# Grouped attention: the output projection as three float32r products per chunk, its operands split by ScalarE and GpSimd

## The chip, the cores and the metric

The kernel runs on one core of a Trainium2 chip. Its engines are TensorE (PE in the profile; its weight loads stand apart as PEld), VectorE (DVE), ScalarE (ACT), GpSimd (POOL) and SyncE (SP, which issues the DMAs). The metric is the device time of one execution in microseconds, as the median of several runs. Lower is better.

## The reference

Sixteen batches of 128 tokens with 256 features pass through six layers, each with a layer norm ahead of it and a residual behind it: causal attention, cross attention, a gated MLP, grouped attention, masked cross attention, and an MLP with quantised operands. The change is in the fourth, `_L1_attn_ref`:

```
D_MODEL, H, G = (256, 32, 8)          # 32 heads of 8 features, 8 groups of keys and values
Q = x @ Wq + bq ; K = x @ Wk + bk ; V = x @ Wv + bv
scores = einsum(Q, K) / sqrt(D_K) ; attn = softmax(scores) ; out = einsum(attn, V)
return out @ Wo + bo                  # the product that the change touches
```

## The kernel before

`grouped_attention` runs between 803 and 995 us of the profiled execution. Each engine has its own program, a function `step(t, s)` that is called for t from -2 to 17. Step t of TensorE works on several batches at once: it projects queries, keys and values of batch t+1, makes the scores of batch t, turns the maxima of the scores (`turn_maxima`, L2623), weighs the values (`weigh_values`, L2652), turns the output of batch t-1 (`turn_out`, L2681, and `turn_heads`, L2695), and projects the heads of batch t-2 (`project_heads`, L2703). The order on each engine is written out by hand; engines wait for each other through semaphores that count batches, and an engine that waits holds up all that stands behind in its own order.

`project_heads(b)` is out @ Wo for one batch: 128 tokens by 256 features, summed over two chunks (EC = 2) of 128 features. Its stationary operand is `headsT`, the turned heads in SBUF, and its moving operand is `wo`. Both are float32, and TensorE's records show each float32 product as two passes (four records in a batch). The path of a batch through it is this:

- VectorE `normalise_heads` (L2544 and L2546) divides by the sums and writes `heads`.
- TensorE `turn_heads` (L2695) turns them into PSUM (`bank_misc`, upper half).
- ScalarE `copy_headsT` (L2458) copies them to SBUF in the same step, t = b+1.
- TensorE `project_heads` (L2703) runs in step t = b+2, behind `turn_maxima(t, s, 1)` and ahead of `turn_out`.
- VectorE `update_x` (L2555) adds the product to x, and `statistics` (L168 to L172) of that batch follow a step later.

On ScalarE a step ends with `own_queries` (L2421) and the next one begins with `copy_keys` (L2439), which waits for TensorE's projections of keys and queries (L2657). On GpSimd a step begins with `add_bias` (L2383), then `narrow_q` (L2367), which waits for ScalarE's queries (L2413), and `narrow_own_keys` (L2375). The last batch, 15, passes `turn_heads` in step 16 and `project_heads` in step 17. Then all engines meet and `masked_cross_attention` begins, with products of weights on TensorE (L1801, then L1806).

In other layers of the same kernel products are already made from float32r halves: an operand is rounded to float32r by ScalarE (high), the rest is what a subtraction leaves (low), and the product is high*high + high*low + low*high. `PARTS = ((0, 0), (0, 1), (1, 0))` lists these pairs.

Of the kernel before, what the change touches and what calls it, by code (L numbers as in the profile page):

```python
# [5 lines left out]
F32 = mybir.dt.float32  # L6
BF16 = mybir.dt.bfloat16
F32R = mybir.dt.float32r
I32 = mybir.dt.int32
HIGH_BITS = -(1 << 12)  # L10
ALU = mybir.AluOpType
ACT = mybir.ActivationFunctionType
AX = mybir.AxisListType

P = 128
# [5 lines left out]
PARTS = ((0, 0), (0, 1), (1, 0))  # L21
EMBED = 256
EC = EMBED // P
# [4 lines left out]
def nonneg(count):  # L28

    return max(count, 0) if isinstance(count, int) else count  # L30
# [72 lines left out]
class Layer:  # L103
# [17 lines left out]
    def sbuf(self, name, shape, dtype=F32):  # L121
        return self.ctx.enter_context(self.nc.sbuf_tensor(f"{self.name}_{name}", shape, dtype))

    def sem(self, name):

        self.used += 1
        return self.core.semaphores[self.parity][self.used - 1]
# [160 lines left out]
def batch_there(b):  # L288
    return not isinstance(b, int) or 0 <= b < BATCHES
# [1984 lines left out]
def grouped_attention(nc, core, dram, next_weights):  # L2274
# [11 lines left out]
    with ExitStack() as ctx:  # L2286
# [25 lines left out]
        reciprocal = sbuf("reciprocal", [P, HEADS])  # L2312
        heads = sbuf("heads", [P, HEADS, D])
        headsT = sbuf("headsT", [P, EC, P])

        bank_scores, bank_scoresT, bank_out, bank_misc = core.banks[0:2], core.banks[2:6], core.banks[6], core.banks[7]
        turned_maxima = [bank_scoresT[0][:, 0:P], bank_scores[0][:, 0:P]]
# [10 lines left out]
        out_filled, outT_ready, out_turned = sem("out_filled"), sem("outT_ready"), sem("out_turned")  # L2328
        heads_chain, heads_ready = sem("heads_chain"), sem("heads_ready")
        headsT_filled, headsT_ready = sem("headsT_filled"), sem("headsT_ready")  # L2330
        left = Statistics(layer, "left", BATCHES - LEFT_BY_QUAD)
        block = ctx.enter_context(nc.Block())

# [18 lines left out]
        @block.gpsimd  # L2352
        def _(pool):
            for s in range(2):
                pool.memset(values[s][:, :], 0.0)
                last = pool.memset(maxima[s][:, :, :, :], 0.0)
            last.then_inc(constants_ready, 1)
            pool.wait_ge(constants_ready, 1)
            for s in range(2):
                last = pool.memset(values_of(s, D, 1), 1.0)  # L2360
            last.then_inc(constants_ready, 1)
            pool.wait_ge(core.constants_loaded, CONSTANTS)

            def narrow_q(b, s):
                pool.wait_ge(q_ready, b + 1)
                pool.wait_ge(scores_filled, nonneg(GROUPS * (b - 1)))
                pool.tensor_tensor(qT_bf[s][:, :, :], qT[:, :, :],  # L2367
                                   core.ones[:, 0:1].unsqueeze(2).to_broadcast([P, EC, P]), ALU.mult)\
                    .then_inc(q_bf_ready, 1)

            def narrow_own_keys(b, s):
                pool.wait_ge(k_ready, b + 1)
                pool.wait_ge(scores_filled, nonneg(GROUPS * (b - 1)))
                for m in range(PER):
                    last = pool.tensor_tensor(kT_bf[s][:, :, m, :], kT[s][:, :, :],  # L2375
                                              own[:, m:m + 1].unsqueeze(2).to_broadcast([P, EC, P]), ALU.mult)
                last.then_inc(k_bf_ready, 1)

            def add_bias(b):

                pool.wait_ge(bias_ready, 1)
                pool.wait_ge(layer.h_ready, b + 1)
                pool.tensor_tensor(core.batch_x(b), core.batch_x(b), bias[:, :], ALU.add).then_inc(bias_added, 1)  # L2383

            def step(t, s):
                if batch_there(t + 1):
                    if t + 1 > 0:
                        add_bias(t + 1)
                    narrow_q(t + 1, 1 - s)
                    narrow_own_keys(t + 1, 1 - s)  # L2390
                    if t + 1 == 0:
                        add_bias(t + 1)
                if batch_there(t - 3) and not left_to_next(t - 3):
                    layer.pool_rstd(pool, t - 3, STATISTICS_STEPS)
                if isinstance(t, int) and t == -1:
                    left.pool_rstd(pool, LEFT_BY_QUAD)
            batches(pool, step)

        @block.scalar
        def _(act):  # L2400
# [53 lines left out]

            def copy_headsT(b):
                act.wait_ge(headsT_filled, b + 1)
                act.wait_ge(layer.y_filled, nonneg(b))
                act.activation(headsT[:, :, :], bank_misc[:, EMBED:2 * EMBED].rearrange("p (c t) -> p c t", c=EC),  # L2458
                               ACT.Copy).then_inc(headsT_ready, 1)

            def normalise(b):
                act.wait_ge(layer.hT_filled, nonneg(b))
# [8 lines left out]
            last.then_inc(wide_ready, 1)  # L2471

            def step(t, s):
                if batch_there(t + 1):
                    copy_keys(t + 1, 1 - s)
                    copy_queries(t + 1)
# [114 lines left out]
        def _(pe):  # L2591
# [105 lines left out]
                last.then_inc(headsT_filled, 1)  # L2697

            def project_heads(b):
                pe.wait_ge(headsT_ready, b + 1)  # L2700
                y = bank_misc[:, 0:EMBED]
                for c in range(EC):
                    last = pe.matmul(y, headsT[:, c, :], wo[:, c, :], start=(c == 0), stop=(c == EC - 1))  # L2703
                last.then_inc(layer.y_filled, 1)

            def step(t, s):
# [531 lines left out]
```

## Time and profile before

| | us |
|---|---|
| median of 3 runs | 1536.37 (1535.61 to 1536.84) |
| the profiled execution | 1536.67 |
| its span in the trace | 1534.4 |
| TensorE busy | 1454.1 (95%) |
| VectorE busy | 1115.4 (73%) |
| ScalarE busy | 978.9 (64%) |
| GpSimd busy | 734.3 (48%) |

TensorE is close to always busy, yet its share says little about one stage: its products are pipelined, so that records overlap, and a step can be bound by a loop through two engines while TensorE's idle time in it looks small. The profiled execution takes 2.3 us more than its span, for what lies around the first and the last instruction. The DMA engines are all but idle in the middle of the stage.

### The profile page before, as it was taken

To read this page: it belongs to the slowest core of one execution; us is meant where nothing else is said; L and a number is where in the kernel's file an instruction comes from. 1 tells how busy PE (TensorE), PEld (TensorE's weight loads), DVE (VectorE), ACT (ScalarE), POOL (GpSimd) and SP (SyncE) were. 2 spreads that over 40 slices of the span, in tenths; PEclk is the share of its full clock that TensorE was granted. 3 is DMA by queue.
4 is the path that set the end of the run, shared out by engine and by line. 5 is a ranking of instruction groups with operands and counts; after the bars stand their busy time and mean duration, and the time that the engine had idled before them with its cause. 6 is when DMAs were issued, how large, how long until landed. Compare 5 with 4: busy or idle time off the path is not lost. (4 is left out here: it accounts for less than half of the span.)

```text
span 1534.4 us, 30706 instructions
## 1 busy us (share of the span) xinstructions
PE 1454.1 (95%) x10384; PEld 1206.1 (79%) x10384; DVE 1115.4 (73%) x2539; ACT 978.9 (64%) x2620; POOL 734.3 (48%) x899
## 2 busy tenths in 40 slices
PE   5999889999999999899998999899999999989998
PEld 2666678888888888688875555489999999867887
DVE  4888668888888887554545777656777777688887
ACT  2777567777777777432325888677777787742222
POOL 3766545555555555232333433213444444457765
PEclk9999999999999999999998999999999999999999
DMA  6000020000000000000003000020000000000000
GB/s 251 2 2 2 15 87 3 5 3 3 5 3 5 4 3 1 23 1 1 1 7 132 1 2 1 9 103 8 9 8 9 8 2 2 1 1 15 14 11 18
DMA packets 15612, 29.84 MB, mean 19 GB/s; under 512 B 1506, under 2 KB 12003, under 8 KB 14691
## 3 DMA queue, kind: packets, MB, share of 16 engines
q1 hardware_dynamic: 15458, 27.89, 5.0%
q8 instruction: 85, 1.39, 0.4%
q14 instruction: 69, 0.56, 0.1%
HBM read 25.79 MB, written 2.10 MB: 18 GB/s over the span
## 5 line engine op out<-in xcount | busy, mean ns | idle before, releaser
L1468 POOL TENSOR_TENSOR weights_even<-weights_even,cross_reciprocal 128x512 f32<-128x512 f32 x64 | 66.7, 1042 | 187.4 <-DVE cross_reciprocal L1720 187.4
L945 POOL TENSOR_TENSOR cross_work<-cross_work,cross_reciprocal 128x512 f32<-128x512 f32 x64 | 66.6, 1040 | 174.8 <-DVE cross_reciprocal L1102 174.8
L1168 PE MATMUL bank<-ident,cross_work 128*128 128x128 f32 x768 | 117.3, 275 | 2.5 <-DVE cross_work L1080 2.2
L998 ACT ACTIVATE cross_work<-bank,cross_shift,cross_q_rms 128x128 f32<-128x128 f32 x256 | 113.6, 456 | 5.2 <-DVE cross_shift L1074 4.5
L1168 PEld LDWEIGHTS bank<-ident,cross_work 128*128 128x128 f32 x768 | 89.9, 141 | 30.1 <-DVE cross_work L1080 21.2
L2525 DVE TENSOR_REDUCE grouped_maxima<-bank 128x4 bf16<-128x512 f32 x128 | 82.3, 685 | 36.4 <-PE bank L2606 36.4
L2001 POOL TENSOR_TENSOR mlp_low_inner<-mlp_inner,mlp_high_inner 128x512 fp32r<-128x512 f32 x36 | 48.7, 1353 | 117.6 <-ACT mlp_high_inner L2044 117.6
L1557 ACT ACTIVATE weights_even<-bank,cross_shift 128x128 f32<-128x128 f32 x256 | 90.4, 366 | 11.1 <-DVE cross_shift L1712 10.0
L1710 DVE TENSOR_REDUCE cross_maxima<-bank 128x4 f32<-128x512 f32 x64 | 44.1, 689 | 71.8 <-PE bank L1854 71.8
L2878 ACT ACTIVATE mx_silu<-bank 128x512 f32<-128x512 f32 x32 | 19.1, 598 | 113.3 <-PE bank L3028 113.3
L404 POOL TENSOR_TENSOR causal_masked_maxima<-causal_maxima,causal_constants 128x512 bf16<-128x512 bf16 x64 | 66.5, 1060 | 46.5 <-DVE causal_maxima L552 42.1
L1193 PE MATMUL bank<-high_weights,cross_high 128*128 128x512 f32 x192 | 87.0, 453 | 0.0
L2404 ACT ACTIVATE grouped_probs<-bank 128x512 f32<-128x512 f32 x128 | 69.9, 606 | 23.5 <-PE bank L2639 23.5
L1885 PE MATMUL bank<-cross_high_wo,cross_high_heads 128*128 128x256 f32 x256 | 76.2, 298 | 8.0 <-DVE cross_low_heads L1699 7.8
L986 ACT ACTIVATE cross_high_probsT<-bank 128x512 fp32r<-128x512 f32 x64 | 38.4, 599 | 67.7 <-PE bank L1168 67.7
L2100 DVE SCALAR_TENSOR_TENSOR mlp_gated<-mlp_tanh,bank 128x512 f32<-128x512 f32 x36 | 24.7, 687 | 77.5 <-ACT mlp_tanh L2038 71.9
L1836 PE MATMUL bank<-cross_high_hT,late_high 128*128 128x256 f32 x256 | 78.0, 305 | 0.7 <-ACT weights_even L1550 0.7
L1258 PE MATMUL bank<-cross_high_wo,cross_high_heads 128*128 128x256 f32 x256 | 77.1, 301 | 0.0
L1193 PE MATMUL bank<-low_weights,cross_high 128*128 128x512 f32 x192 | 76.6, 399 | 0.0
L1193 PE MATMUL bank<-high_weights,cross_low 128*128 128x512 f32 x192 | 76.6, 399 | 0.0
L1885 PE MATMUL bank<-cross_high_wo,cross_low_heads 128*128 128x256 f32 x256 | 72.3, 282 | 0.0
L1885 PE MATMUL bank<-cross_low_wo,cross_high_heads 128*128 128x256 f32 x256 | 72.3, 282 | 0.0
(382 smaller groups left out, 5362.2 us busy)
## 6 DMA issues: line engine op xcount, KB each, us to landing
weights_even<-in_weights SPq DMA_DIRECT2D x2, 2560.0 KB, 11.6
weights_even<-in_weights SPq DMA_DIRECT2D x2, 1732.0 KB, 8.5
weights_odd_early<-in_weights SPq DMA_DIRECT2D x1, 3072.0 KB, 11.8
weights_odd_values<-in_weights SPq DMA_DIRECT2D x1, 3072.0 KB, 18.8
weights_odd_late<-in_weights SPq DMA_DIRECT2D x2, 1536.0 KB, 9.5
x<-in_x SPq DMA_DIRECT2D x4, 512.0 KB, 8.0
out<-mx_result SPq DMA_DIRECT2D x16, 128.0 KB, 1.7
weights_even<-in_weights SPq DMA_DIRECT2D x2, 512.0 KB, 5.8
```

The costliest lines, as they stand in the source:

```text
L404: pool.tensor_tensor(masked_maxima[g][:, :, :], maxima[s][:, g, :].unsqueeze(2).to_broadcast([P, PER, P]), later.unsqueeze(1).to_broadcast ...
L945: pool.tensor_tensor(probs[x], probs[x], reciprocal[x][:, :].unsqueeze(2).to_broadcast([P, PER, P]), ALU.mult).then_inc(probs_divided, 1)
L998: last = act.activation(probs[x][:, j, :], bank_scores[:, j * P:(j + 1) * P], ACT.Exp, scale=q_rms[x][:, j:j + 1], bias=shift[x][:, j:j + ...
L1168: last = pe.transpose(bank[:, j * P:(j + 1) * P], source, core.ident[:, :])
L1193: last = pe.matmul(out, half[:, c, :], split_weights[b][:, at:at + PER * D], start=(k == 0), stop=(k == len(jobs) - 1))
L1258: last = pe.matmul(bank_y[:, 0:EMBED], heads[x][a][:, j, :], wo_split[c][:, h, :], start=(g == 0 and m == 0), stop=(g == GROUPS - 1 and m ...
L1468: pool.tensor_tensor(probs[x], probs[x], reciprocal[x][:, :].unsqueeze(2).to_broadcast([P, JOBS, P]), ALU.mult).then_inc(probs_divided, 1)
L1557: last = act.activation(probs[x][:, j, :], bank_scores[x][:, j * P:(j + 1) * P], ACT.Exp, scale=SCALE, bias=shift[x][:, j:j + 1], accum_ou ...
L1836: last = pe.matmul(bank_q[:, j * BOTH * P:(j + 1) * BOTH * P], wqk_split[b][:, c, h * D:(h + 1) * D], hT[s][a][:, c, :, :].rearrange("p b ...
L1885: last = pe.matmul(bank_y[s][:, k * EMBED:(k + 1) * EMBED], heads[x][a][:, k * PER + j, :], wo_split[b][:, g * PER + j, :], start=(g == 0 ...
L2404: act.activation(probs[:, SLOTS * c + j, :], bank_scoresT[j][:, :], ACT.Exp, scale=SCALE)\
L2525: dve.tensor_reduce(maxima[s][:, c, 2 * pair + j, 0:PER], bank_scores[j].rearrange("p (h k) -> p h k", h=PER), AX.X, ALU.max).then_inc(max ...
```

## The change

The edit adds four SBUF tensors (high and low halves of the turned heads and of `wo`, in float32r) and four semaphores. ScalarE rounds `wo` once at the start of step 0 and GpSimd subtracts it at the start of step 1. For each batch ScalarE rounds `headsT` from SBUF at the start of step b+2, ahead of that step's `copy_keys`; GpSimd subtracts at the start of the same step, ahead of `add_bias` and `narrow_q`; TensorE's `project_heads(b)` waits for GpSimd and makes six float32r products in place of two float32 ones. `copy_headsT` waits for the previous subtraction in place of the previous product.

```diff
+        headsT_split = [sbuf(f"{half}_headsT", [P, EC, P], F32R) for half in ("high", "low")]
+        wo_split = [sbuf(f"{half}_wo", [P, EC, EMBED], F32R) for half in ("high", "low")]
...
+            def low_wo():
+                pool.wait_ge(wo_high, 1)
+                pool.tensor_tensor(wo_split[1][:, :, :], wo, wo_split[0][:, :, :].bitcast(F32), ALU.subtract)\
+                    .then_inc(wo_low, 1)
+
+            def low_headsT(b):
+                pool.wait_ge(headsT_high, b + 1)
+                pool.tensor_tensor(headsT_split[1][:, :, :], headsT[:, :, :], headsT_split[0][:, :, :].bitcast(F32),
+                                   ALU.subtract).then_inc(headsT_low, 1)
+
             def step(t, s):
+                if isinstance(t, int) and t == 1:
+                    low_wo()
+                if batch_there(t - 2):
+                    low_headsT(t - 2)
                 if batch_there(t + 1):
...
             def copy_headsT(b):
                 act.wait_ge(headsT_filled, b + 1)
-                act.wait_ge(layer.y_filled, nonneg(b))
+                act.wait_ge(headsT_low, nonneg(b))
...
+            def round_headsT(b):
+                act.wait_ge(headsT_ready, b + 1)
+                act.wait_ge(layer.y_filled, nonneg(b))
+                act.activation(headsT_split[0][:, :, :], headsT[:, :, :], ACT.Copy).then_inc(headsT_high, 1)
...
             def step(t, s):
+                if isinstance(t, int) and t == 0:
+                    act.activation(wo_split[0][:, :, :], wo, ACT.Copy).then_inc(wo_high, 1)
+                if batch_there(t - 2):
+                    round_headsT(t - 2)
                 if batch_there(t + 1):
                     copy_keys(t + 1, 1 - s)
...
             def project_heads(b):
-                pe.wait_ge(headsT_ready, b + 1)
+                if isinstance(b, int) and b == 0:
+                    pe.wait_ge(wo_low, 1)
+                pe.wait_ge(headsT_low, b + 1)
                 y = bank_misc[:, 0:EMBED]
-                for c in range(EC):
-                    last = pe.matmul(y, headsT[:, c, :], wo[:, c, :], start=(c == 0), stop=(c == EC - 1))
+                jobs = [(c, x, w) for c in range(EC) for x, w in PARTS]
+                for m, (c, x, w) in enumerate(jobs):
+                    last = pe.matmul(y, headsT_split[x][:, c, :], wo_split[w][:, c, :],
+                                     start=(m == 0), stop=(m == len(jobs) - 1))
                 last.then_inc(layer.y_filled, 1)
```

## Rows read from the trace of the kernel before

**Rows 1.** Windows: us, busy (records) of PE, PEld, DVE, ACT, POOL, then PEclk, DMA.

```profile
915.00:935.00 20.00, 19.57 (x157) 10.31 (x155) 15.77 (x37) 16.20 (x41) 8.28 (x14) 1.00 0.01 2
```

**Rows 2.** Timeline of TensorE, one step: start, duration, line, tiles, count, idle time.

```profile
919.60 0.22 PE L2623 MATMUL bank<-minus_ident_bf,grouped_maxima 128*128 128x128 bf16 x1
919.66 1.08 PE L2703 MATMUL bank<-weights_odd_late,grouped_headsT 128*128 128x256 f32 x4
920.58 0.60 PE L2681 MATMUL bank<-ident,grouped_outT 128*128 128x128 f32 x4
922.50 0.44 PE L2687 MATMUL bank<-ident,grouped_h 128*128 128x128 f32 x2
922.77 0.38 PE L2695 MATMUL bank<-ident,grouped_heads 128*128 128x128 f32 x2
...
930.19 0.22 PE L2623 MATMUL bank<-minus_ident_bf,grouped_maxima 128*128 128x128 bf16 x1
```

**Rows 3.** Timeline of VectorE, the same step.

```profile
919.86 0.69 DVE L2534 TENSOR_TENSOR grouped_shifts<-bank,grouped_columns 128x512 bf16<-128x512 f32 x1 [0.33 <-PE bank L2623]
...
921.50 0.42 DVE L2555 TENSOR_TENSOR x<-x,bank 128x256 f32<-128x256 f32 x1
...
922.23 0.42 DVE L2546 TENSOR_TENSOR grouped_heads<-bank,grouped_reciprocal 128x256 f32<-128x256 f32 x1
```

**Rows 4.** Timeline of ScalarE and of GpSimd, where the added work goes.

```profile
925.18 0.95 ACT L2421 ACTIVATE grouped_q_own<-grouped_qT,grouped_columns 128x256 f32<-128x256 f32 x2
926.73 0.62 ACT L2439 ACTIVATE grouped_kT<-bank,grouped_columns 128x128 f32<-128x128 f32 x2 [0.60 <-issue]
...
927.95 0.61 POOL L2367 TENSOR_TENSOR grouped_qT_bf<-grouped_qT,ones 128x256 bf16<-128x256 f32 x1 [5.15 <-ACT grouped_qT L2413]
```

**Rows 5.** One line each: a split of 128x256 by ScalarE and GpSimd elsewhere.

```profile
L1581 ACT ACTIVATE cross_high_context<-cross_context x8: 412/427/434, 1010.4 to 1270.1; 128x256 fp32r<-128x256 f32 x8
L1497 POOL TENSOR_TENSOR cross_low_context<-cross_context,cross_high_context x8: 725/730/734, 1010.9 to 1297.6; 128x256 fp32r<-128x256 f32 x8
```

**Rows 6.** Timeline of TensorE, 256-column float32r products of another layer.

```profile
1102.93 0.38 PE L1885 MATMUL bank<-cross_high_wo,cross_high_heads 128*128 128x256 f32 x1
1103.16 0.28 PE L1885 MATMUL bank<-cross_low_wo,cross_high_heads 128*128 128x256 f32 x1
...
1103.87 0.28 PE L1885 MATMUL bank<-cross_low_wo,cross_high_heads 128*128 128x256 f32 x1
```

**Rows 7.** Timeline of ScalarE at the stage's start.

```profile
821.87 0.62 ACT L2439 ACTIVATE grouped_kT<-bank,grouped_columns 128x128 f32<-128x128 f32 x2 [3.84 <-issue]
```

**Rows 8.** Timeline of TensorE and ScalarE, step 16, batch 14.

```profile
989.24 1.13 PE L2703 MATMUL bank<-weights_odd_late,grouped_headsT 128*128 128x256 f32 x4
989.46 0.60 ACT L2446 ACTIVATE grouped_outT<-bank 128x512 f32<-128x512 f32 x1 [1.26 <-PE bank L2652]
```

**Rows 9.** Timeline of three engines, batch 15 and the next layer's start.

```profile
992.25 0.38 ACT L2458 ACTIVATE grouped_headsT<-bank 128x256 f32<-128x256 f32 x1 [2.20 <-PE bank L2695]
992.69 1.13 PE L2703 MATMUL bank<-weights_odd_late,grouped_headsT 128*128 128x256 f32 x4 [0.47 <-ACT grouped_headsT L2458]
993.92 0.42 DVE L2555 TENSOR_TENSOR x<-x,bank 128x256 f32<-128x256 f32 x1 [1.33 <-issue]
994.92 1.35 PE L1801 MATMUL bank<-weights_even 128*128 128x128 f32 x10 [1.09 <-DVE x L2555]
```

**Rows 10.** Windows around a fall of the clock, and around this stage's end.

```profile
800.40:804.20 3.80, 1.74 (x13) 1.56 (x14) 1.63 (x5) 0.81 (x3) 1.06 (x4) 1.00 0.00 0
804.20:811.00 6.80, 6.80 (x24) 5.46 (x24) 0.00 (x0) 1.14 (x4) 0.21 (x3) 0.50 0.96 371
992.00:995.40 3.40, 1.83 (x10) 1.19 (x9) 1.36 (x10) 0.45 (x2) 0.65 (x2) 1.00 0.00 0
995.40:1002.20 6.80, 6.80 (x63) 6.80 (x63) 4.82 (x10) 5.48 (x13) 0.00 (x0) 1.00 0.79 249
```

**Rows 11.** Timeline of TensorE inside the stretch at the half clock.

```profile
807.67 3.57 PE L2657 MATMUL bank<-grouped_hT,weights_odd_late 128*128 128x128 f32 x16
```

More of the change, by code:

```diff
@@ L2330, in grouped_attention @@
         headsT_filled, headsT_ready = sem("headsT_filled"), sem("headsT_ready")
+        headsT_high, headsT_low = sem("headsT_high"), sem("headsT_low")
+        wo_high, wo_low = sem("wo_high"), sem("wo_low")
         left = Statistics(layer, "left", BATCHES - LEFT_BY_QUAD)
```

## The prediction

> **What bounds the kernel now.** I read the busy time by stretch first, then the timelines of one step in the middle of the stage, engine by engine, then those of its two ends, and last the granted clock around the stage's borders. The stretch in the middle shows TensorE busy 19.57 of 20 us at the full clock, VectorE 15.77, ScalarE 16.20 [rows 1]. That looks like a stage bound by TensorE, in which every saved product pays. The timeline says something else. A step lasts 10.59 us (`turn_maxima` starts at 919.60 and again at 930.19), and in it `project_heads` starts at 919.66 and the next thing at 920.58, so the product costs 0.92 us of TensorE's time [rows 2]. But VectorE starts a run of work at 919.86, released by that same `turn_maxima` ahead of the product: shifts, statistics, `update_x` at 921.50, the reciprocal, and the heads from 922.23 to 922.65 [rows 3]. `turn_heads` needs those heads and starts at 922.77, right behind `turn_h`, which started at 922.50 [rows 2]. So two chains arrive there almost together: TensorE's own, and VectorE's, which begins at `turn_maxima` and doesn't contain the product. The reader is to see that the wait is hidden in the rows because both are in step, not because VectorE is early: TensorE's second product of `turn_h` began about 0.11 us before 922.77, so VectorE's 922.65 left under 0.12 us minus the semaphore's way.
>
> **The product.** Four passes of 0.92 us go. Six float32r products of the same 256 columns come: six intervals of such a series take 1103.87 - 1103.16 = 0.71 us when it runs, and with the slower first interval 1103.87 - 1102.93 = 0.94 us for seven, or some 0.82 for six [rows 6]. I take 0.76 us, a saving of 0.16 us a step on TensorE (0.10 to 0.21). Then `turn_out`, the scores and `turn_h` all come 0.16 us earlier and `turn_heads` stands waiting for heads at 922.65, which haven't moved: `update_x` is held by the statistics ahead of it on VectorE, not by the product. What gets through is only what TensorE lost between the heads' arrival and 922.77. Bounds: 0, and the whole 0.16. The heads' end and that start are 0.12 us apart, and a semaphore takes part of that (0.05 us from the copy's end at 992.64 to the product at 992.69 [rows 9]), so I take 0.015 us a step, over some 13 full steps 0.2 us gained; the upper end is 13 x 0.16 = 2.1 us.
>
> **The rounding and the subtraction, in full steps.** ScalarE's round of 128x256 from SBUF takes 0.43 us and GpSimd's subtraction 0.73 us [rows 5]. The round goes behind `own_queries` (two in 0.95 us, done at 926.13) and ahead of `copy_keys`, before which ScalarE idles 0.60 us [rows 4]; since operations overlap by about a tenth, it occupies 0.40 and ends near 926.5, with `copy_keys` still at 926.73. Behind it on ScalarE stand the keys, the queries and the exponentials; if the cover were gone each would be later by the excess, and GpSimd's `narrow_q` and TensorE's scores with them. The subtraction runs from 926.55 to 927.3 in GpSimd's idle 5.15 us before `narrow_q` at 927.95 [rows 4]. Its other new waits (the previous `y_filled`, the previous low half) were met a step before. TensorE's wait for the low half comes at 930.25, 3 us later. I charge nothing; between 0 and 0.2 us a step is what I can't exclude. SP's queue and its DMAs aren't passed or changed. `wo` is split once: ScalarE idles 3.84 us before the keys in step 0 [rows 7], which hides a 128x512 round (estimate from the 128x256 one: at most 0.86), and GpSimd's subtraction (at most 1.46, by the same doubling) has its wait before the next `narrow_q`.
>
> **The end of the stage: batch 14.** ScalarE idles 1.26 us until `copy_outT` at 989.46 [rows 8]. The round starts as that idle time does, near 988.0 to 988.2 with its overlap, and takes 0.43; the subtraction's 0.73 [rows 5] ends between 989.1 and 989.4, and TensorE reaches the product at 989.24 [rows 8]: no delay, or 0.2 us that the product's own saving pays back. In these last steps TensorE and ScalarE, not VectorE, set the pace, so the 0.16 us saved on batch 13 does arrive: another 0.2 us gained.
>
> **The end of the stage: batch 15.** Nothing stands beside it. Now: the copy ends at 992.64, the product starts at 992.69 and its result is there at 993.82, VectorE adds at 993.92, the next layer's first product starts at 994.92 [rows 9]. After: copy to 992.64, round 0.43 with 0.05 ahead of it to 993.12, GpSimd 0.07 + 0.73 to 993.92, then 0.05, and six products with a cold start: five starts after the first at 0.23 + 4 x 0.118 = 0.70, and 0.28 for the last [rows 6], so 0.98, to 994.95. That is 1.1 us later than 993.82 (0.9 to 1.3), and everything behind it moves by that.
>
> So far: -0.2 - 0.2 + 1.1 = +0.7 us.
>
> **The clock behind that gap.** The granted clock stays at 2.4 GHz here: TensorE is busy 1.83 of 3.40 us in 992.0 to 995.4 and the next 6.8 us are at 1.00 [rows 10]. At the stage's other border it was busy 1.74 of 3.80 us (800.4 to 804.2), and the next 6.8 us ran at half, 1.2 GHz [rows 10]. The change stretches the same border: between `turn_heads`' end (992.2) and the next layer at 994.92 + 1.1 = 996.0, TensorE would have 0.98 us of records in 3.8 us where it had 1.13 in 2.7. That is less than it did ahead of that fall (26% of the time against 46%, where it now has 54%), so I expect a fall. Its price: at half the 16 products of 128 columns take (3.57 - 0.37)/15 = 0.21 us each [rows 11], in the next layer (1.35 - 0.35)/9 = 0.11 [rows 9]. TensorE is busy 6.80 of 6.80 us there [rows 10], so nothing hides it: 6.8 us at half do the work of 3.5, a loss of 3.3 us, less up to half of the idle 1.1 us if the fall comes ahead of the restart (2.7 to 3.3). I take 3.2.
>
> The Trainium skill ("TensorE: Matmul & The Clock Gate", section "HAM oscillation — how this bites in real kernels") speaks of a re-throttle only for idle gaps longer than any in this border, so by it there is no fall and the sum stays at +0.7. This trace disagrees: ahead of the fall at 804.2 the 1.74 us of busy time left TensorE no such gap either.
>
> **Sum.** 1536.67 (the profiled execution, 1534.4 of span and 2.3 around it) + 0.7 + 3.2 = 1540.6. The median of the runs is 0.3 below the profiled execution, so 1540.3.
>
> **Rivals.**
> - *No fall of the clock.* The same schedule, with the next layer at 2.4 GHz throughout: 1536.37 + 0.7 = 1537.1 (1536.6 to 1537.6), no measurable change. For it: the clock held at this very border before [rows 10], and one other border is thin evidence. Against it: this border becomes emptier than that one. It decides at the next layer's first products, which cost 0.11 us each or 0.21. This is my case on the other side, not slower.
> - *TensorE's saving counts.* If the heads were there in time after all, 13 steps give 0.16 each: 1537.1 - 1.9 = 1535.2, still within the noise; at 0.21 a step and no fall 1534.6. For it: TensorE's 19.57 of 20 us [rows 1]. Against it: VectorE's chain starts ahead of the product [rows 3].
> - *The cover is too thin.* ScalarE's keys slip, by some 0.2 us a step (a round that takes 0.80 in place of 0.43, or products that come with more than the 0.12 us of rows 6): 13 x 0.2 = 2.6 us on top, 1542.9. Against it: 0.60 us of idle time for 0.40 of work, and the exponentials wait for TensorE behind it anyway.
>
> **How the numbers follow.** The forecast gets 0.66 with 1539.3 to 1541.1 as its own range, no fall 0.23, the saving 0.05, the thin cover 0.06. A measurement of this kernel tells 0.2%, 3.1 us, from no change. Of the forecast about a tenth lies under +3.1 (a tail of 0.9 and a price of 2.7), so slower gets 0.60 + 0.05 = 0.65; the same 0.23 + 0.06 + 0.03 = 0.32; faster 0.03. The range takes in both clock cases: 1536.4 (no fall and a small tail) to 1541.6.
>
> **What would show it.** In the step: six records of `project_heads` in about 0.76 us, then an idle time before `turn_heads` with VectorE's heads as its releaser, and the step still 10.57 to 10.59 us; an even 10.43 would prove the saving counts. ScalarE's idle time before `copy_keys` falls from 0.60 to about 0.2 and no more. At the end: the product of batch 15 at about 994.0, the next layer at about 996.0, and a granted clock of 0.5 for 6.8 us near its start. With the clock at 1.00 there, the forecast is wrong and the first rival right; with steps over 10.7 us, the third.

## The result, and the profile after

The changed kernel takes 1541.38 us in the median of 20 runs (1537.18 to 1543.29). The kernel before, run beside it, takes 1536.85 us (20 runs, 1532.49 to 1540.28). The ratio of the two is 1.0026, 95% interval 1.0018 to 1.0034: slower by 0.26%, little but clear of the noise. The forecast was 1540.3.

The first view is TensorE's timeline of one full step (start, duration, engine, line, tiles, shape, count, idle time before):

```profile
921.12 0.22 PE L2650 MATMUL bank<-minus_ident_bf,grouped_maxima 128*128 128x128 bf16 x1
921.15 0.36 PE L2733 MATMUL bank<-grouped_high_wo,grouped_high_headsT 128*128 128x256 f32 x1
921.35 0.28 PE L2733 MATMUL bank<-grouped_low_wo,grouped_high_headsT 128*128 128x256 f32 x1
...
921.83 0.28 PE L2733 MATMUL bank<-grouped_high_wo,grouped_low_headsT 128*128 128x256 f32 x1
921.95 0.60 PE L2708 MATMUL bank<-ident,grouped_outT 128*128 128x128 f32 x4
923.87 0.44 PE L2714 MATMUL bank<-ident,grouped_h 128*128 128x128 f32 x2
924.23 0.44 PE L2722 MATMUL bank<-ident,grouped_heads 128*128 128x128 f32 x2
924.60 1.06 PE L2679 MATMUL bank<-grouped_probs,grouped_values 128*32 128x512 f32 x8
925.60 0.39 PE L2633 MATMUL bank<-grouped_kT_bf,grouped_qT_bf 32*128 32x512 bf16 x2
925.91 1.60 PE L2684 MATMUL bank<-grouped_hT,weights_odd_late 128*128 128x128 f32 x12
927.40 0.23 PE L2650 MATMUL bank<-minus_ident_bf,grouped_maxima 128*128 128x128 bf16 x1
...
931.67 0.22 PE L2650 MATMUL bank<-minus_ident_bf,grouped_maxima 128*128 128x128 bf16 x1
```

The product takes 921.95 - 921.15 = 0.80 us where it took 0.92 [rows 2], and `turn_h` comes 0.15 us sooner behind `turn_maxima` (2.75 us for 2.90). But `turn_heads` now comes 0.36 us behind `turn_h`, where it was 0.27. (The profile prints no idle time there, because the records of `turn_h` end only at 924.31; the wait is read from the starts.) The step is 931.67 - 921.12 = 10.55 us for 10.59. VectorE in the same step:

```profile
921.38 0.69 DVE L2561 TENSOR_TENSOR grouped_shifts<-bank,grouped_columns 128x512 bf16<-128x512 f32 x1 [0.32 <-PE bank L2650]
...
923.03 0.42 DVE L2582 TENSOR_TENSOR x<-x,bank 128x256 f32<-128x256 f32 x1
923.37 0.35 DVE L2571 RECIPROCAL grouped_reciprocal<-bank 128x32 f32<-128x32 f32 x1
923.75 0.42 DVE L2573 TENSOR_TENSOR grouped_heads<-bank,grouped_reciprocal 128x256 f32<-128x256 f32 x1
924.09 1.28 DVE L2552 TENSOR_REDUCE grouped_maxima<-bank 128x4 bf16<-128x512 f32 x2
```

It hasn't moved: 1.65 us from the shifts to `update_x`, as in 921.50 - 919.86 = 1.64 before [rows 3]. The heads are ready at 923.75 + 0.42 = 924.17, and `turn_heads` follows at 924.23. ScalarE and GpSimd take the added work in idle time (the first two lines are ScalarE's, the last three GpSimd's):

```profile
927.36 0.45 ACT L2482 ACTIVATE grouped_high_headsT<-grouped_headsT 128x256 fp32r<-128x256 f32 x1
928.22 0.62 ACT L2457 ACTIVATE grouped_kT<-bank,grouped_columns 128x128 f32<-128x128 f32 x2 [0.41 <-issue]
...
927.89 0.73 POOL L2396 TENSOR_TENSOR grouped_low_headsT<-grouped_headsT,grouped_high_headsT 128x256 fp32r<-128x256 f32 x1 [4.26 <-ACT grouped_high_headsT L2482]
928.57 0.73 POOL L2387 TENSOR_TENSOR x<-x,grouped_bias 128x256 f32<-128x256 f32 x1
929.44 0.61 POOL L2371 TENSOR_TENSOR grouped_qT_bf<-grouped_qT,ones 128x256 bf16<-128x256 f32 x1
```

At the end of the stage nothing covers it. In order of time, four engines:

```profile
995.02 0.41 PE L2722 MATMUL bank<-ident,grouped_heads 128*128 128x128 f32 x2 [1.00 <-DVE grouped_heads L2573]
995.46 0.38 ACT L2476 ACTIVATE grouped_headsT<-bank 128x256 f32<-128x256 f32 x1 [2.17 <-PE bank L2722]
995.88 0.42 ACT L2482 ACTIVATE grouped_high_headsT<-grouped_headsT 128x256 fp32r<-128x256 f32 x1
996.37 0.72 POOL L2396 TENSOR_TENSOR grouped_low_headsT<-grouped_headsT,grouped_high_headsT 128x256 fp32r<-128x256 f32 x1 [3.32 <-ACT grouped_high_headsT L2482]
997.15 0.58 PE L2733 MATMUL bank<-grouped_high_wo,grouped_high_headsT 128*128 128x256 f32 x1 [1.72 <-POOL grouped_low_headsT L2396]
...
998.38 0.41 PE L2733 MATMUL bank<-grouped_high_wo,grouped_low_headsT 128*128 128x256 f32 x1
998.89 0.42 DVE L2582 TENSOR_TENSOR x<-x,bank 128x256 f32<-128x256 f32 x1 [3.10 <-issue]
999.88 1.41 PE L1801 MATMUL bank<-weights_even 128*128 128x128 f32 x5 [1.09 <-DVE x L2582]
```

From `turn_heads` to the next layer's first product it is 999.88 - 995.02 = 4.86 us, where it was 994.92 - 991.81 = 3.11. The turn in the kernel before (its copy and what follows are in [rows 9]):

```profile
991.81 0.41 PE L2695 MATMUL bank<-ident,grouped_heads 128*128 128x128 f32 x2 [1.00 <-DVE grouped_heads L2546]
```

In the changed kernel the products here are 0.21 us apart and not 0.12: the clock falls at 997.2, as they begin. The windows (us, busy and records of PE, PEld, DVE, ACT, POOL, then PEclk, DMA share, GB/s):

```profile
993.80:997.20 3.40, 0.68 (x5) 0.25 (x3) 1.89 (x9) 0.80 (x2) 0.83 (x2) 1.00 0.00 0
997.20:1004.00 6.80, 5.71 (x25) 5.45 (x26) 1.87 (x7) 1.52 (x3) 0.50 (x2) 0.50 0.34 87
1004.00:1010.00 6.00, 6.00 (x55) 5.97 (x54) 4.46 (x8) 4.60 (x12) 0.00 (x0) 1.00 0.99 374
```

TensorE was busy 0.68 of 3.40 us at 2.4 GHz; then come 6.8 us at 1.2 GHz. Before, at this border, it was busy 1.83 of 3.40 and kept 2.4 GHz [rows 10].

The two profiled executions differ by 7.1 us of span. Of that 2.0 lies ahead of the stage (its first `turn_maxima` is at 822.83 for 820.85). 0.3 of it is there by 26 us, and the rest goes with a stretch of 3.4 us at half clock at 171 us that only the changed kernel's execution had; the edit changes nothing there, so this is chance. The stage, from that `turn_maxima` to the next layer, is 177.05 us for 174.07. Of these 3.0 us the border is 1.75, and the full steps give some 0.5 back. Most of what is left comes from another fall, 6.8 us long, at 980.1: in step 15 the second `turn_maxima` follows the first by 5.62 us where it was 4.01. The profiled execution of the kernel before has no fall there, though the same kernel with other small edits does (e2, e5, e11). Behind the stage 541.6 us remain to the end of the span for 539.5. And the time around the span is 1.8 us (1543.27 less 1541.5), where it was 2.3.

### The profile page after: what moved, and what is told of

It reads as the page before. It is cut to its first block and busy times, and to the rows that moved or that the text cites. A ratio compares the mean times of both kernels' runs of the same rounds, so it can differ in the third digit from the quotient of the medians.

```text
span 1541.5 us, 30821 instructions
## 1 busy us (share of the span) xinstructions
PE 1461.0 (95%) x10416; PEld 1210.4 (79%) x10416; DVE 1116.0 (72%) x2539; ACT 984.3 (64%) x2637; POOL 748.0 (49%) x916
```

## The experiments

The runs come in four groups, the changed kernel's and three of experiments (e1, e2, e3 and e7; e4, e5, e6 and e8; e9 to e12), the last of them on another chip than the two before it. The kernel before was run in each, and the ratios in the table are to those runs. Its means in the groups are 1536.9, 1537.6, 1537.4 and 1537.4 us, so where an experiment is set against the changed kernel, which is in a group of its own, up to 0.7 us can come from that.

One kernel's executions spread over 4 to 13 us. Most of that goes with one quantity that every run lists: from its granted clock c the time at half clock is 2 x (1 - c) x span. Over the 234 executions for which the clock is listed, of all kernels, one slope fits: each us at half clock goes with 0.26 us of time, with 1.2 us left over. So the table gives a mean time at equal half clock beside the median, with twice its standard error; it is a fit, not a measurement. Two things blur it. The clock's record begins 13 to 26 us into an execution, and what is ahead of it isn't counted: in all 14 profiles the products of 512 columns between 18 and 22 us come 0.85 us apart, as at half clock (0.43 from 30 us on), but only the ten records that begin by 15 us count a stretch there. And the time around the span is 1.8 us for the changed kernel, e1 to e4 and e7 to e10 (2.0 for e6), but 2.3 for the kernel before, e5, e11 and e12: 0.5 us that belongs to no step. By spans alone the changed kernel stands at +1.0 and not +0.5. "Step" is the period of `turn_maxima` in the middle, "border" the time from the last `turn_heads` to the next layer's first product, "rest" from there to the end of the span; these three are of the profiled execution.

```
kernel                          runs  median   ratio (95%)             step   border  rest    at half, mean  equal half, to before
before                            88  1537.27                          10.59  3.11    539.5   31.7            0
changed                           20  1541.38  1.0026 (1.0018-1.0034)  10.55  4.86    541.6   41.7           +0.5 (0.6)
e1 last batch float32             12  1539.54  1.0016 (1.0003-1.0028)  10.56  3.10    540.2   39.0            0.0 (0.7)
e2 before, split of batch 15      11  1540.54  1.0020 (1.0009-1.0032)  10.59  4.36    541.2   36.9           +1.5 (0.7)
e3 TensorE kept busy              12  1537.70  1.0005 (0.9993-1.0018)  10.56  4.40    540.0   32.5           +0.5 (0.7)
e7 all splits, float32 products   12  1540.47  1.0020 (1.001-1.003)    10.59  4.35    542.5   35.6           +1.8 (0.7)
e6 products without splits        12  1540.33  1.0012 (0.9997-1.0028)  10.56  2.95    542.7   40.5           -0.4 (0.7)
e4 changed, heads first            6  1547.21  1.0061 (1.004-1.0081)   11.06  4.20    541.2   37.6           +7.8 (1.0)
e5 before, heads first             7  1545.42  1.0050 (1.0032-1.0068)  11.20  3.11    539.7   33.1           +7.6 (0.9)
e8 e4 with e1                      6  1545.74  1.0050 (1.003-1.007)    11.06  3.11    541.1   39.6           +6.4 (1.0)
e9 changed, statistics cut        12  1538.96  1.0009 (0.9995-1.0023)  10.47  4.21    541.3   36.4           -0.1 (0.7)
e11 before, statistics cut        12  1537.83  0.9998 (0.9984-1.0013)  10.62  3.10    539.8   32.0           +0.1 (0.7)
e12 before, last steps kept busy  12  1537.67  1.0001 (0.9987-1.0015)  10.59  3.11    539.5   31.0            0.0 (0.7)
e10 e9 + e1 + e12                 12  1536.18  0.9994 (0.9982-1.0006)  10.47  3.30    539.9   33.8           -1.7 (0.7)
```

**e1: the changed kernel, batch 15 by the old products.** The serial split at the border is gone; all else stays. (In the diffs from here on, notes behind # are added, and conditions that only pick the steps are not shown.)

```diff
-                if batch_there(t - 2):
+                if batch_there(t - 2) and t - 2 != BATCHES - 1:    # round_headsT and low_headsT
...
+                if b == BATCHES - 1:                               # project_heads: the two float32 products
```

> The changed kernel, but batch 15 alone goes the old way: two float32 products straight from headsT, no round and no subtraction for it. Theory (serial end plus clock): the 1.2 us between the last copy_headsT and the last product shrink to 0.05, the border looks as it did before the change, the clock falls there as seldom as before, and the time is that of the kernel before, less 0.4 to 0.7 us: ratio to before 0.9990 to 1.0005. Rival (the loss is spread over the steps, through the added ScalarE and GpSimd work): the time stays that of the change, 1.0025 to 1.0035 of before.

The border is back at 3.10 us and the clock holds behind it (rest 540.2). The median comes 1.8 us down, not all the way to the kernel before: the ratio's interval, 1.0003 to 1.0028, lies above what was expected. This kernel still had 7.3 us more at half clock than the kernel before (95% interval 2.8 to 11.8), and not measurably less than the changed kernel (2.7, interval -2.5 to 8.0).

**e2: the kernel before, with the round, the subtraction and the wait for batch 15 alone; its products stay float32.** The split of `wo` at the stage's start stays in too.

```diff
+                if t - 2 == BATCHES - 1:       # ScalarE: round_headsT, GpSimd: low_headsT
+                if b == BATCHES - 1:           # TensorE
+                    pe.wait_ge(headsT_low, 1)
```

> The kernel before (float32 products everywhere), but for batch 15 alone ScalarE rounds headsT, GpSimd subtracts, and the product, still float32 from headsT, waits for that; its results are not used. Theory: the last product starts 1.2 us later, at 993.9 by the clock of the trace before, the next layer 1.2 us later, and the clock falls to 1.2 GHz near that point in most executions for 6.8 us: +1.2 without a fall, +4.4 with one, a median of +3.5 to +4.5 us. Rival (only the serial work costs, the clock's falls are chance): a median of +1.2 us and falls at that place no more often than before.

One operation more on each of two engines, at the end of the stage, costs 1.25 us at the border (4.36 for 3.11) and is followed by a fall (3.4 us long, rest 541.2). The split of `wo` costs next to nothing: one early step is 0.05 us longer. The median is 3.1 us above that of the kernel before in the same group, most of what the whole change costs. The time at half clock is 5.3 us longer (interval 1.5 to 9.1), which by the fit is 1.4 us of it. Its chain, to compare with [rows 9]:

```profile
993.27 0.42 ACT L2482 ACTIVATE grouped_high_headsT<-grouped_headsT 128x256 fp32r<-128x256 f32 x1
993.76 0.72 POOL L2396 TENSOR_TENSOR grouped_low_headsT<-grouped_headsT,grouped_high_headsT 128x256 fp32r<-128x256 f32 x1 [5.63 <-ACT grouped_high_headsT L2482]
994.54 1.13 PE L2734 MATMUL bank<-weights_odd_late,grouped_headsT 128*128 128x256 f32 x4 [1.72 <-POOL grouped_low_headsT L2396]
995.77 0.42 DVE L2582 TENSOR_TENSOR x<-x,bank 128x256 f32<-128x256 f32 x1 [2.59 <-issue]
996.77 4.41 PE L1801 MATMUL bank<-weights_even 128*128 128x128 f32 x24 [1.09 <-DVE x L2582]
```

**e3: the changed kernel, with TensorE kept busy at the border** by transposes that nothing reads.

```diff
+                if t == BATCHES + 1:
+                    keep_busy(14)
                 if batch_there(t - 2):
                     project_heads(t - 2)
+                if t == BATCHES + 1:
+                    keep_busy(8)
```

> The changed kernel, with 14 transposes of the identity on TensorE ahead of the wait for the last product and 8 behind it, into a bank that nobody reads any more: they fill the idle time and do nothing for the output. Theory: the last product still starts 1.2 us late (the 14 take 1.55 us of the 1.7 that TensorE waits), but the clock no longer falls at this border: +0.5 to +1.2 us against before, 3 less than the change; the profile shows 1.00 from 990 to 1005. Rival (the falls come from elsewhere): no shorter than the change, +4 to +5 us.

The serial chain is all there (border 4.40, where e9 below has 4.21 at full clock), yet the clock stays up. TensorE's timeline, then the windows:

```profile
994.32 1.69 PE L2728 MATMUL bank<-ident 128*128 128x128 f32 x14
...
996.20 0.39 PE L2737 MATMUL bank<-grouped_high_wo,grouped_high_headsT 128*128 128x256 f32 x1 [0.20 <-POOL grouped_low_headsT L2396]
...
997.02 1.04 PE L2728 MATMUL bank<-ident 128*128 128x128 f32 x8
998.47 2.80 PE L1801 MATMUL bank<-weights_even 128*128 128x128 f32 x23 [0.41 <-PEq L2286]
```

```profile
993.00:996.40 3.40, 2.20 (x18) 1.93 (x18) 1.74 (x9) 0.80 (x2) 0.97 (x2) 1.00 0.00 0
996.40:999.80 3.40, 2.99 (x26) 2.78 (x26) 1.18 (x6) 0.76 (x2) 0.35 (x2) 1.00 0.06 16
```

Against the changed kernel the median falls by 3.7 us (the means by 2.4, 95% interval 1.0 to 3.9), although the transposes add 0.2 us to the border; each set against the kernel before of its own group, the means differ by 3.1. At equal half clock it stands where the changed kernel does, +0.5; the whole gain is in the clock, 9.2 us less at half. So it is shown that the clock costs this kernel time and that work at the border gives it back, by an edit that takes no work away. It isn't shown that the split alone brings the falls: e1, which takes the split away, keeps 6.4 us more at half clock than e3 (interval 0.9 to 12.0).

**e7: the changed kernel's splits with the old products.**

```diff
-                jobs = [(c, x, w) for c in range(EC) for x, w in PARTS]
...
+                for c in range(EC):
+                    last = pe.matmul(y, headsT[:, c, :], wo[:, c, :], start=(c == 0), stop=(c == EC - 1))
```

> The changed kernel with all its rounds, subtractions and waits, but the two float32 products from headsT and wo in place of the six; the halves are made and not used. Theory: the step lasts as before, 10.59 us (10.58 to 10.60), since ScalarE and GpSimd do the new work in idle time; the end of the stage costs 1.2 to 1.3 us and the clock falls there: +3.5 to +5 us against before. Rival (rounding and subtracting slow the steps): a step of 10.65 us or more.

The step is 10.59, as before the change, with all rounding and subtracting in it: the cover is complete. The border is 4.35, as in e2, and so is the time: 3.0 us over the kernel before in the median, a little less than expected, with 4.0 us more at half clock (interval 0.8 to 7.1).

**e6: the changed kernel's six products without the splits.** The stationary operand is a half of `wo`; this leaves the values of the turned heads out of the output.

```diff
-                    last = pe.matmul(y, headsT_split[x][:, c, :], wo_split[w][:, c, :],
+                    last = pe.matmul(y, wo_split[x][:, c, 0:P], wo_split[w][:, c, :],
```

> The six float32r products alone: no round and no subtraction per batch, the stationary operands are taken from the split wo (in place of the turned heads, whose values this leaves out of the output), and the product waits for copy_headsT as before. Theory: the step is that of the change, 10.55 us, so the per-batch splitting is free in the steps; the end has no added 1.2 us, the last product ends 0.2 us sooner than before, and the clock falls at the border as in the kernel before: -0.6 to -1.0 us against before. Rival (per-batch splitting costs in the steps): a step shorter than 10.50 us.

The step is 10.56 and the border 2.95, 0.16 us shorter than before: there the shorter product arrives in full. The median is 3.1 us over the kernel before (the ratio's interval, 0.9997 to 1.0028, just reaches 1), where 0.6 to 1.0 us less was expected, with 8.8 us more at half clock (interval 4.4 to 13.3). Its profile has a fall at the border although the border is short. So the serial split isn't the only thing that brings falls here: the short products alone go with more of them, and the expectation had nothing for that.

**e4 and e5: VectorE's heads ahead of its statistics,** in steps up to 14, in the changed kernel and in the kernel before, to take away the wait of `turn_heads`.

```diff
-                if batch_there(t - 3) and not left_to_next(t - 3):
-                    statistics(t - 3)
                 if batch_there(t - 2):
                     update_x(t - 2)
                 if batch_there(t - 1):
                     normalise_heads(t - 1)
+                if batch_there(t - 3) and not left_to_next(t - 3):
+                    statistics(t - 3)
```

> The changed kernel with VectorE's order turned in steps up to 14: update_x and normalise_heads ahead of the statistics. The heads come some 0.9 us earlier. Theory (TensorE's saved 0.16 us a step is absorbed by the wait for the heads): now it counts, the step goes from 10.55 to 10.42 to 10.45 us, and the time is 1.3 to 1.7 us less than the change. Rival (something else bounds the step): the step stays at 10.55.

> The kernel before with the same order of VectorE as in the heads-first kernel, float32 products. Theory: TensorE's own chain already reaches turn_heads at the same moment as the heads did, so earlier heads bring nothing: a step of 10.57 to 10.59 us and the time of before within 0.4 us. Rival (VectorE alone bounds the step): the step falls below 10.5 us here too.

Both are slower by 8 us and more, which the expectations missed. VectorE in e4:

```profile
922.72 0.42 DVE L2582 TENSOR_TENSOR x<-x,bank 128x256 f32<-128x256 f32 x1 [0.58 <-ACT grouped_values L2447]
...
923.44 0.42 DVE L2573 TENSOR_TENSOR grouped_heads<-bank,grouped_reciprocal 128x256 f32<-128x256 f32 x1
...
924.82 1.29 DVE L2552 TENSOR_REDUCE grouped_maxima<-bank 128x4 bf16<-128x512 f32 x2
```

`update_x` isn't free until 922.72: it also waits for ScalarE's copy of the values (L2447), and that copy waits for the product. So VectorE idles 0.58 us in the place of the statistics, and these then stand ahead of the row maxima, which end at 926.11. TensorE waits for them (0.58 us idle before its next scores at 926.17). In the changed kernel the statistics fill just that idle time. The pair does show one thing well: where `update_x` waits for that copy, the product is in VectorE's chain. The copy starts 1.32 us behind `turn_maxima` in e5 and 1.18 in e4, and 11.20 - 11.06 = 0.14 us of the saving arrive in each step. And with the heads early TensorE reaches `turn_heads` by itself 3.18 us behind `turn_maxima` with the float32 product (e5) and 3.03 with the new one (e4); in the kernel before and the changed kernel the distances are 3.17 and 3.11. TensorE's way was the later one before, VectorE's is now.

**e8: e4 with e1.** 

> Heads-first order together with the old way for batch 15: the step's saving counts and the end costs nothing. Theory: 13 steps x 0.15 us saved, the end as before: -2.0 to -2.6 us against before, falls of the clock at the border as often as in the kernel before, and faster than both kernels. Rival: no better than the old way for batch 15 alone (-0.4 to -0.7).

The border is 3.11 and the time stays as slow as the step. The expectation, faster than both kernels, missed with e4's. Against e4 it is 1.5 us less both in the medians and at equal half clock, near the border's 4.20 - 3.11 = 1.09.

**e9 and e11: only the first instruction of the statistics stays ahead,** the short ones go behind the next row maxima; in the changed kernel and in the kernel before.

```diff
                 if batch_there(t - 3) and not left_to_next(t - 3):
-                    statistics(t - 3)
+                    first_statistics(t - 3)
...
                 if batch_there(t + 1):
                     row_maxima(t + 1, 1 - s, 0, 0)
+                if batch_there(t - 3) and not left_to_next(t - 3):
+                    rest_of_statistics(t - 3)
```

> The changed kernel, with VectorE's statistics of batch t-3 cut in two in the full steps: only their first instruction stays ahead of update_x, the short ones go behind the next row maxima. Theory: in the changed kernel a step is set by VectorE's unbroken run from turn_maxima over the shifts, statistics, update_x and the heads to the row maxima (3.11 us to turn_heads); update_x could start 0.31 us sooner (922.72 for 923.03, as with the heads first), the row maxima end earlier, and the next bound is TensorE's own way with the shorter product, 3.03 us. So the step goes from 10.55 to 10.47 us, 1.0 us over the stage, 1539.5 to 1540.5 in all. Rival: the product's saving can't pass at all, because ScalarE or the keys set the step: it stays at 10.55. Other rival: the short instructions behind the row maxima delay the next ones, as whole statistics there did: 10.6 or more.

> The kernel before with the same cut of the statistics. Theory: there the float32 product stands on TensorE's own way to turn_heads and to ScalarE's copies (3.17 us, 3.18 with the heads first), so that earlier heads give nothing: the step stays at 10.58 to 10.60 us, ratio 0.999 to 1.001. With e9 this is a table of two by two: only where both are done does the step fall to 10.47. Rival: VectorE sets the step in the kernel before already, and it falls by 0.08 there too.

The step is 10.47 in e9, as forecast to the hundredth, and 10.62 in e11. TensorE in e9:

```profile
919.32 0.22 PE L2671 MATMUL bank<-minus_ident_bf,grouped_maxima 128*128 128x128 bf16 x1
...
922.07 0.44 PE L2735 MATMUL bank<-ident,grouped_h 128*128 128x128 f32 x2
922.35 0.38 PE L2743 MATMUL bank<-ident,grouped_heads 128*128 128x128 f32 x2
```

`turn_heads` comes 922.35 - 919.32 = 3.03 us behind `turn_maxima`, right behind `turn_h`. The same edit gives -0.08 us with the shorter product and +0.03 with the long one: each shortens one of two parallel ways, and only both together shorten the step. (e11's 0.03 are more than I expected; there the next row maxima start 0.06 us later behind the scores than in the kernel before, 0.51 for 0.45.) At the border, here wholly at 2.4 GHz, it is 4.21: 1.10 us more than before. The median, 1538.96, is half a us below what was expected; the run isn't shown to be slower than the kernel before, nor faster.

**e12: the kernel before, with TensorE kept busy in steps 15 and 16.**

```diff
+                if t == BATCHES - 1:
+                    pe.wait_ge(headsT_ready, t - 1)
+                    keep_busy(bank_misc, 12)
+                if t == BATCHES:
+                    keep_busy(bank_scores[1], 8)
```

> The kernel before, with transposes that nothing reads in TensorE's idle time of the last steps: 12 in step 15 where the projections were, 8 at the start of step 16. Theory: most executions have a stretch at 1.2 GHz that begins 976 to 984 us in, behind this thinner step; with TensorE kept busy it goes, for 1.5 to 2.5 us on the median, less 0.2 for the longer step 15: ratio 0.9985 to 1.000. Rival: the stretches come at about a fixed distance from the earlier ones, whatever TensorE does here: one is still seen between 976 and 984 us and the ratio is 1.000 to 1.001.

No fall is seen between 976 and 988 us, and none in e10 either, where ten of the twelve other profiles have one (the kernel before and e7 don't). Yet neither median nor time at half clock moved (31.0 for 31.7), and the ratio is the rival's. One profile without a fall doesn't show that the transposes took one away, since the profile of the kernel before has none there either.

**e10: the changed kernel with e9, e1 and e12 together.**

> What the runs so far point to, together: the changed kernel with batch 15 by float32 products (no serial split at the border), the statistics cut in two, and the transposes of e12. Theory: step 10.47, the border as in the kernel before (2.65 us from the copy of batch 15 to the next layer), fewer stretches at 1.2 GHz: 1.6 us less by steps, up to 2 by the clock, so 1533.5 to 1536, ratio 0.9975 to 0.9990 to the kernel before. Rival: the stretches go elsewhere, and it is at 1536 to 1538.

It has the lowest median, 1536.18, 5.2 us under the changed kernel (the means 4.3, 95% interval 3.1 to 5.5), but not the 1536 or less that was expected; it lies where the rival put it. Against the kernel before its interval, 0.9982 to 1.0006, still reaches over 1, so it isn't shown to be faster. At equal half clock it is 1.7 us better, about what the shorter steps (13 x 0.12 us) make. Its border is 3.30 and not 3.11: the next layer's first product comes 1.19 us behind `update_x` and not 1.00, for a reason that no run shows.

## Why the prediction was right, point by point

- **The product, 0.76 us for 0.92.** Nearly. It is 0.80: the first interval is 0.20 us and the others 0.12. The saving is 0.12 to 0.15 us.
- **TensorE's saving stops at the heads: 0.015 us a step.** Right in mechanism: `turn_heads` follows the heads by 0.06 us in the changed kernel, and e9 shows that it is they that hold the rest. The size was under: 0.04 us. I had read one chain too few. In the kernel before, the keys' projection waits for ScalarE's copy of the turned heads, behind exponentials that themselves stand behind the product (the copy ends at 924.37, the projection starts at 924.51). In the changed kernel that copy starts 4.22 us behind `turn_maxima`, where it was 4.36, and the projection no longer waits for it: it follows the scores ahead of it by 0.31 us, where it was 0.42. With that way shorter, VectorE's, just behind it, took over. Over the stage this is some 0.5 us against my 0.2.
- **The splits cost nothing in full steps.** Right: 10.59 in e7, 10.56 in e6 and 10.55 with both. ScalarE still idles 0.41 us ahead of the keys, where I expected 0.2.
- **Batch 14, 0.2 us gained.** Nearly: from `turn_maxima` of step 15 to `turn_heads` of batch 15 the distance is 8.88 us before (982.92 to 991.81), 9.00 with the splits alone (e7), and 8.77 and 8.78 in e1 and e3: 0.1 gained. The splits take 0.1 here, and the products pay it back.
- **Batch 15, +1.1 us.** Right: 1.10 at full clock (e9). With the float32 product it is 1.25 (e2). In the profiled execution of the changed kernel it is 1.75, because the clock fell ahead of the product: the other 0.65 us belong to the next item.
- **The fall behind the border, 3.2 us.** The profile has it where I put it, 6.8 us long. Its size there: rest is 539.5 to 540.2 us in the seven profiles without a fall there (before, e1, e3, e5, e10, e11, e12), 541.1 to 541.3 in four with 3.4 us (e2, e4, e8, e9) and 542.5 and 542.7 in two with 6.8 (e7, e6). So 6.8 us at half cost about 2.7 (2.3 to 3.2), 3.4 us about 1.4, and not each execution has the long form. In the changed kernel it is 2.1 behind the next layer's start and 0.65 ahead of it, also near 2.7. I had 3.2, with TensorE busy through all of the 6.8 us; it was busy for 5.71 of them. (A price holds for its place: e5 and e12 have a fall of 3.4 us near 1370 us too, inside their rest, and are no longer for it.) All five profiles with the serial split and no transposes have a fall behind the border (changed, e2, e4, e7, e9), and of the eight without the split two (e6, e8); e3, with both split and transposes, has none. The term was priced for one execution that surely falls, and set against a median. Per execution the split is worth less: e2 and e7 have 5.3 and 4.0 us more at half clock than the kernel before, 1.0 to 1.4 us of time by the fit.
- **The sum, +3.9 us.** Measured: +4.5 in the medians. The fit parts it into +0.5 us of schedule (I had +0.7) and +2.6 of clock, from 10 us more at half (interval 6.5 to 13.6). The two make the difference of the means, +3.2 against all 88 runs of the kernel before; against the 20 of its own group it is +3.8. The median shows more than the mean, because 16 of the changed kernel's 20 executions had 40 us or more at half clock and it lies among them. The sum also had 2.3 us around the span, which measured 1.8.
- **In part luck.** The clock's share came out near the forecast's 3.2, but not from the border alone, as the forecast had it. The split accounts for 1.0 to 1.4 us (e2, e7). The short products account for as much or more: with a border as before, e1 and e6 have 7.3 and 8.8 us more at half clock, 1.9 and 2.3 us by the fit. The prediction has no term for that; it made up for a border term that was too large.

The rule of the Trainium skill weighed in the prediction ("TensorE: Matmul & The Clock Gate", section "HAM oscillation — how this bites in real kernels") would have given no fall, since no idle gap is as long as it asks. The changed kernel's trace disagrees: TensorE's longest idle time ahead of the fall is 1.72 us.

What stays open: why the kernels with six short products in each step have more time at half clock even where the border is as before (e1 39.0, e6 40.5 us against 31.7), why the transposes of e3 bring the time at half clock down to 32.5, and whether those of e12 took a fall away at all. One profile for each kernel shows where its falls were once; for the other executions only the sum is known.

## What to carry to other kernels

Before you count a saved product, find every way that leads around the loop and its length: here TensorE's and ScalarE's, VectorE's and the next bound lay within 0.15 us of each other, so that of 0.15 us 0.04 arrived, and another 0.08 once VectorE's work was cut to fit. Work that steady steps hide stands bare at the last batch: leave it out there (e1), since one round and one subtraction cost 1.1 to 1.25 us in line, and about as much again through the clock (1.0 to 1.4 us by the fit, e2 and e7). And compare such small effects only with the time at half clock beside each run.

## What the runs showed of the hardware

- With TensorE kept busy by products that nothing reads, across a wait of 1.7 us, the profiled execution stayed at 2.4 GHz there, and the kernel was faster by 2.4 us in the mean (e3, interval 1.0 to 3.9).
- A fall comes in two lengths, 3.4 and 6.8 us, in the same place of nearly the same kernel (e7 6.8 at 994.4; e9 3.4 at 995.9).
- The spread of one kernel's executions, 1532.5 to 1546.0 for the kernel before, goes mostly with the time in such stretches: its runs list 12 to 59 us at half clock, which accounts for 0.8 of the variance.
- With short float32r products in place of the float32 ones and the border as before, a kernel has 7 to 9 us more at half clock (e1 7.3, e6 8.8), though the products take TensorE 0.80 us a step and not 0.92. Why isn't known.
- A float32r product of 256 columns takes 0.12 us at the full clock and 0.21 at half; the float32 one that it replaces takes 0.23 a pass, so three of the one against two passes of the other save an eighth to a fifth (0.72 to 0.80 for 0.92).
